# Local attention in a two-block transformer kernel: scores of two heads alternate between the array halves, VectorE adds the mask together with the maximum, and scale vectors move into the rotary tables

## The reference

```python
h = shift_token(x)                       # half the channels come from the token before
q, k, v = split(h @ wqkv)                # 8 heads of 64
q = l2norm(q) * qs; k = l2norm(k) * ksc  # t / clip(norm(t), 1e-12)
q = q * cos * scale + rotate_half(q) * sin * scale
k = k * cos / scale + rotate_half(k) * sin / scale
# windows of 128 tokens; the keys are the window before and the window itself
sim = einsum('bhwid,bhwjd->bhwij', q * 8.0, keys)
sim = where((i < j) | (i > j + 128) | (j == -1), -max_float, sim)
o = einsum('bhwij,bhwjd->bhwid', softmax(sim), values)
x = x + o @ wo
h = layernorm(shift_token(x)) * lg + lb
a, g = split(h @ w1 + b1)
x = x + (a * gelu(g)) @ w2 + b2
```

## Time and profile before

| | us |
|---|---|
| median of 3 runs | 3386.52 (3385.89 to 3389.96) |
| the profiled execution, its own time | 3379.02 |
| its span, first to last instruction | 3377.2 |
| busy: PE / PEld | 3182.4 / 2050.2 |
| busy: DVE / ACT / POOL | 2572.0 / 2144.2 / 764.8 |
| mean granted TensorE clock | 0.973 |

### The profile page before, as it was taken

One profiled execution on the slowest core, in us unless ns is written; L12 is line 12 of the kernel. 1 busy time (PEld: TensorE's weight loads), 2 busy tenths in 40 slices (PEclk: granted clock), 3 DMA queues, 4 the chain that ended last, 5 costly groups with the idle time before them and its releaser, 6 DMA issues. The chain is left out here.

```text
span 3377.2 us, 56295 instructions
## 1 busy us (share of the span) xinstructions
PE 3182.4 (94%) x20728; PEld 2050.2 (61%) x20792; DVE 2572.0 (76%) x4114; ACT 2144.2 (63%) x4870; POOL 764.8 (23%) x954
## 2 busy tenths in 40 slices
PE   8979999999999999999859999999999999999996
PEld 5633333333333333333448888888888888888885
DVE  4578888888888888886357777777777777777774
ACT  3417777777777777777745555555555556565563
POOL 4500000000000000000343333333334343343341
PEclk9959999999999999999979999999999999999998
DMA  3322222222222222222400000000000000000001
GB/s 116 129 50 39 39 38 38 38 38 38 38 38 38 34 36 32 33 38 29 144 32 1 1 0 0 0 0 0 0 1 34 1 0 0 0 0 0 0 1 68
DMA packets 47027, 97.95 MB, mean 29 GB/s; under 512 B 17184, under 2 KB 29472, under 8 KB 40480
## 3 DMA queue, kind: packets, MB, share of 16 engines
q1 hardware_dynamic: 42400, 95.48, 15.1%
q10 hardware_dynamic: 4544, 1.38, 0.2%
HBM read 71.13 MB, written 25.69 MB: 29 GB/s over the span
## 5 line engine op out<-in xcount | busy, mean ns | idle before, releaser
L653 DVE TENSOR_REDUCE mx<-aux 128x1 f32<-128x1024 f32 x1024 | 1203.6, 1219 | 169.0 <-PE aux L528 168.8
L623 ACT ACTIVATE probs<-scores 128x512 f32<-128x512 f32 x2048 | 1062.9, 604 | 312.1 <-PE scores L552 308.9
L528 PE MATMUL aux<-k_stack,q_stack 48*128 48x512 f32 x2048 | 815.1, 476 | 31.6 <-DMA k_stack<-qk_dram 18.2
L552 PE MATMUL scores<-q_stack,k_stack 50*128 50x512 f32 x2048 | 756.4, 450 | 50.7 <-ACT probs L623 24.6
L552 PEld LDWEIGHTS scores<-q_stack,k_stack 50*128 50x128 f32 x2048 | 342.7, 186 | 602.6 <-ACT probs L623 549.6
L563 PE MATMUL pv<-probs,v_ones 128*32 128x512 f32 x4096 | 551.3, 610 | 1.4 <-ACT probs L623 0.7
L528 PEld LDWEIGHTS aux<-k_stack,q_stack 48*128 48x128 f32 x2048 | 345.3, 191 | 132.9 <-DVE mx L653 68.6
L1186 PE MATMUL bank<-QO,w_sb 128*128 128x128 f32 x2816 | 333.5, 278 | 0.9 <-ACT QO L1267 0.9
L1186 PEld LDWEIGHTS bank<-QO,w_sb 128*128 128x128 f32 x2816 | 321.3, 193 | 12.1 <-issue 10.3
L494 POOL CAST m_parts<-head_max 128x16 fp32r<-128x16 f32 x32 | 6.3, 196 | 1370.8 <-DVE head_max L658 1370.8
L1199 PE MATMUL bank<-kT,wqkv_sb 64*128 64x128 f32 x1984 | 288.6, 285 | 9.5 <-issue 0.4
(11 more groups left out here) (172 smaller groups left out, 4667.7 us busy)
## 6 DMA issues: line engine op xcount, KB each, us to landing
q_stack<-qk_dram SPq DMA_DIRECT2D x192, 128.0 KB, 5.0
k_stack<-qk_dram SPq DMA_DIRECT2D x192, 128.0 KB, 6.9
qk_dram<-qkT_hi SPq DMA_DIRECT2D x32, 256.0 KB, 3.1
qk_dram<-qkT_lo SPq DMA_DIRECT2D x32, 256.0 KB, 3.6
out<-x_sb SPq DMA_DIRECT2D x9, 384.0 KB, 4.1
wqkv_sb<-in_wqkv SPq DMA_DIRECT2D x2, 1536.0 KB, 7.4
w_sb<-in_w SPq DMA_DIRECT2D x2, 1408.0 KB, 11.3
x_sb<-in_x SPq DMA_DIRECT2D x1, 2048.0 KB, 18.8
```

The source lines that it names most:

```text
L528: last = nc.tensor.matmul(aux[:, ring["unit"], block_of_keys % 2], q_stack[rows, r % BODY, tile * P:(tile + 1) * P], k_stack[rows, r % BOD ...
L552: nc.tensor.matmul(scores[:, item % BANKS1], k_stack[0:SCORE_ROWS, r % BODY, s * P:(s + 1) * P], q_stack[0:SCORE_ROWS, r % BODY, j * 512:( ...
L623: nc.scalar.activation(probs[:, item % PROBS], scores[:, item % BANKS1], ACT.Exp, scale=float(D1) ** -0.5).then_inc(probs_ready, 1)
L653: nc.vector.reduce_max(mx[:, slot, tile, half:half + 1], aux[:, unit].rearrange("p a k -> p (a k)"), AX.X).then_inc(max_taken, 1)
```

## The change

- **Scores.** The mask matmul goes. A matmul has one head against 256 keys at once, if there are two blocks. Banks are filled in pairs: a head in rows 0 to 63 into one bank, then a head in rows 64 to 127 into the other, and again. `PAIRS` is ordered for it, and kT and v keep the keys of a sequence so that both blocks are one access.
- **Mask and maximum.** For each head DVE computes (score + mask) times the inverse norm of q into `probs`, with the running minimum as second output (`tensor_tensor_reduce`). q's scale is -8 instead of 8, so the minimum is the negated maximum. ACT takes the exponential from SBUF, with scale -1.
- **Rotary.** POOL builds cosine and sine tables that hold the scale vectors, once for each pair of tiles (a position serves both sequences). DVE multiplies q and k from PSUM with the cosine table, so the separate cosine product goes. ACT copies q and k to SBUF before it squares them, and POOL's sine products wait for that copy and no longer for the norms. Only k is multiplied with its inverse norm. Before the combining adds DVE has an explicit drain.

```diff
@@ mask_and_shift
+    for keys in (slice(0, P), slice(2 * P, 3 * P)):
+        nc.gpsimd.affine_select(out=mask_sb[:, keys], in_=mask_sb[:, keys], compare_op=ALU.is_ge, fill=NO_KEY,
+                                base=0, pattern=[[1, P]], channel_multiplier=-1)
...
-NO_KEY = -1e30
-PAIRS = ((0, 2), (4, 6), (1, 3), (5, 7))
+NO_KEY, NO_SCORE = 1e30, 3e38
+PAIRS = ((0, 2), (1, 3), (4, 6), (5, 7))
@@ gpsimd
+            def rotary_tables(place, layer, position):
+
+                by_half = lambda a: a.rearrange("p a (s d) -> p a s d", s=2)
+                for table, source, scales, made in ((cos_table, cos_sb, qks_sb, cos_table_made), (sin_table, sin_sb, qks_swapped, sin_table_made)):
+                    nc.gpsimd.tensor_tensor(out=by_half(table[:, place]), in0=source[:, position].unsqueeze(2).to_broadcast([P, 2, 2, D2 // 2]),
+                                            in1=by_half(scales[:, layer]), op=ALU.mult).then_inc(made, 1)
...
-                    w.upto(norm2_made, t + 3)
+                    if st.tile_of_pair(2) == 0:
+                        w.upto(sin_table_made, st.pair(2) + 1)
+                    w.upto(qk_copied, 2 * (t + 3))
...
-                                                in1=sin_sb[:, st.position(2)].unsqueeze(2).to_broadcast([P, 2, H2, D2 // 2]),
+                                                in1=sin_table[:, st.table(2), :, lo:lo + D2 // 2].unsqueeze(2).to_broadcast([P, 2, H2, D2 // 2]),
                                                 op=ALU.mult).then_inc(sin_rnorm_made, 1)
+                    w.upto(norm2_made, t + 3)
...
+                if st.exists(3) and st.tile_of_pair(3) == 0:
+                    rotary_tables(st.table(3), st.layer(3), st.position(3))
@@ tensor
-                    for j in range(4):
-                        out = begin(f"S{j}", t + 1)
-                        nc.tensor.matmul(out[:], identb[:], mask_sb[:].rearrange("p a k -> p (a k)"), start=True, stop=False, skip_group_check=True)
-                        for u, h in enumerate(PAIRS[j]):
-                            rows = slice(h % 2 * D2, (h % 2 + 1) * D2)
-                            for kb in range(1 if st.first(1) else 0, 2):
-                                last = nc.tensor.matmul(out[:, (2 * u + kb) * P:(2 * u + kb + 1) * P], qT[rows, h // 2, :],
-                                                        kT[rows, st.slot(1 if kb else -1), h // 2, :], start=False, stop=(u == 1 and kb == 1), skip_group_check=True)
-                        end(last, f"S{j}")
+                    blocks = st.key_blocks(1)
+                    n_keys = P * len(blocks)
+                    for both in ((0, 1), (2, 3)):
+                        outs = [begin(f"S{j}", t + 1) for j in both]
+                        for u in range(2):
+                            for j, out in zip(both, outs):
+                                h = PAIRS[j][u]
+                                rows = slice(h % 2 * D2, (h % 2 + 1) * D2)
+                                at = 2 * u * P + blocks[0] * P
+                                last = nc.tensor.matmul(out[:, at:at + n_keys].rearrange("p (b k) -> p b k", k=P), qT[rows, h // 2, :],
+                                                        kT[rows, st.slot(1) % 2, blocks[0]:blocks[-1] + 1, h // 2, :], start=True, stop=True)
+                                if u == 1:
+                                    end(last, f"S{j}")
@@ scalar
                         src = item(name, t + 2)
+                        nc.scalar.copy(qk[:, a], src[:]).then_inc(qk_copied, 1)
                         nc.scalar.activation(squares[:, a], src[:], ACT.Square).then_inc(squares_made, 1)
...
-                            last = nc.scalar.activation(probs[:, j, u, b0:], src[:, u * 2 * P + b0:(u + 1) * 2 * P], ACT.Exp,
+                            last = nc.scalar.activation(probs[:, j, u, keys], probs[:, j, u, keys], ACT.Exp, scale=-1.0,
                                                         bias=negmax[:, j, u:u + 1], accum_out=sums[:, j, u:u + 1])
@@ vector
-                        nc.vector.tensor_tensor(qk[:, a].rearrange("p (h d) -> p h d", d=D2), bank(name)[:].rearrange("p (h d) -> p h d", d=D2),
-                                                qks_sb[:, st.layer(2), a].unsqueeze(1).to_broadcast([P, H2, D2]), ALU.mult).then_inc(by_dve, 1)
+                        nc.vector.tensor_tensor(qk_cos[:, a].rearrange("p (h d) -> p h d", d=D2), bank(name)[:].rearrange("p (h d) -> p h d", d=D2),
+                                                cos_table[:, st.table(2), a].unsqueeze(1).to_broadcast([P, H2, D2]), ALU.mult).then_inc(by_dve, 1)
...
-                    w.upto(sin_rnorm_made, 3 * (t + 2) + 1)
-                    nc.vector.tensor_tensor(qk_cos[:].rearrange("p a (h d) -> p a h d", d=D2 // 2), qk[:].rearrange("p a (h d) -> p a h d", d=D2 // 2),
-                                            cos_sb[:, st.position(2)].unsqueeze(2).to_broadcast([P, 2, 2 * H2, D2 // 2]), ALU.mult).then_inc(cos_made, 1)
+                    dve.drain().then_inc(cos_made, 1)
...
+                    nc.vector.tensor_tensor(qk_rot[:, 0], qk_cos[:, 0], qk_sin[:, 0], ALU.add)
+                    nc.vector.tensor_tensor(qk_cos[:, 1], qk_cos[:, 1], qk_sin[:, 1], ALU.add).then_inc(rot_made, 1)
...
-                        nc.vector.tensor_reduce(negmax[:, j], src[:, :, P if st.first(1) else 0:], AX.X, ALU.max, negate=True).then_inc(max_made, 1)
+                            last = nc.vector.tensor_tensor_reduce(out=probs[:, j, u, at:at + n_keys], in0=src[:, 2 * u * P + at:2 * u * P + at + n_keys],
+                                                                  in1=mask_sb[:, mask_at:mask_at + n_keys], scale=rnorm[:, st.slot(1, 2), h:h + 1], scalar=NO_SCORE,
+                                                                  op0=ALU.add, op1=ALU.min, accum_out=negmax[:, j, u:u + 1])
+                        last.then_inc(max_made, 1)
...
-                        nc.vector.tensor_tensor(qk_rot[:].rearrange("p a (h d) -> p (a h) d", d=D2), qk_cos[:].rearrange("p a (h d) -> p (a h) d", d=D2),
-                                                rnorm[:].unsqueeze(2).to_broadcast([P, 2 * H2, D2]), ALU.mult).then_inc(rotary_done, 1)
+                        nc.vector.tensor_tensor(qk_rot[:, 1].rearrange("p (h d) -> p h d", d=D2), qk_cos[:, 1].rearrange("p (h d) -> p h d", d=D2),
+                                                rnorm[:, st.slot(2, 2), H2:].unsqueeze(2).to_broadcast([P, H2, D2]), ALU.mult).then_inc(rotary_done, 1)
```

More of the change, by code:

```diff
@@ L70, in slot, with current, key_blocks, tile_of_pair @@
         return (self.t + d) % n
+    def current(self, d):
+        return self.slot(d) // 2
+    def key_blocks(self, d):
+        return (self.current(d),) if self.first(d) else (0, 1)
+    def tile_of_pair(self, d):
+        return (self.t + self.skipped + d) % 2
+    def table(self, d):
+        return (self.t + self.skipped + d) // 2 % 2
+    def pair(self, d):
+        return (self.t + d) // 2
 class Waiter:
@@ L1024, in feed_forward_phase @@
         squares_made, norm2_made, sin_rnorm_made = sem("squares_made"), sem("norm2_made"), sem("sin_rnorm_made")
+        qk_copied, scales_made, cos_table_made, sin_table_made = (sem(n) for n in ("qk3_copied", "scales_made", "cos_table_made", "sin_table_made"))
         cos_made, rot_made = sem("cos3_made"), sem("rot3_made")
@@ L1046, in _ @@
             w.on(norm2_made, 1), w.on(hmv_made, 1)
-            w.on(norm2_floor, 1), w.on(var_made, 1)
+            w.on(norm2_floor, 1), w.on(var_made, 1), w.on(qk_copied, 2)
+            w.on(sin_table_made, 1, lambda step: step.exists(2) and step.tile_of_pair(2) == 0)
             w.on(fmv_made, 1, last_layer(-2)), w.on(fvar_made, 1, last_layer(-2))
@@ L1138, in _ @@
                         for u in range(2):
-                            for kb in range(1 if st.first(0) else 0, 2):
+                            for kb in st.key_blocks(0):
                                 last = nc.tensor.transpose(out[:, (2 * u + kb) * P:(2 * u + kb + 1) * P], probs[:, j, u, kb * P:(kb + 1) * P], ident[:])
@@ L1169, in _ @@
                     out = begin("oT", t)
+                    blocks = st.key_blocks(0)
                     for c in range(4):
-                        for kb in range(1 if st.first(0) else 0, 2):
+                        for kb in blocks:
                             for half in range(2):
@@ L1174, in _ @@
                                 last = nc.tensor.matmul(out[half * D2:(half + 1) * D2, c * P:(c + 1) * P],
-                                                        v_sb[:, st.slot(0 if kb else -2), (2 * c + half) * D2:(2 * c + half + 1) * D2], PT[:, j, u, kb],
-                                                        start=(kb == 0 or st.first(0)), stop=(kb == 1), tile_position=(0, half * D2))
+                                                        v_sb[:, st.slot(0) % 2 + 2 * kb, (2 * c + half) * D2:(2 * c + half + 1) * D2], PT[:, j, u, kb],
```

(9 more changed lines are left out.)

51 lines of the change are left out of this document (29 added, 22 removed).

## The result

| | before | after |
|---|---|---|
| median, us | 3386.81 (3385.89 to 3389.96, 4 runs) | 3256.26 (3249.47 to 3260.75, 4 runs) |
| ratio to before, 95% interval | | 0.9611 (0.9592 to 0.963) |
| span of the profiled execution | 3377.2 | 3247.7 |
| one tile on TensorE in the first layer | 25.03 | 23.04 to 23.06 |

The kernel became 130.6 us faster; 185 were forecast. The gain arose in the forecast place, the score stage. Three tenths of it did not arrive, because of a wait that the forecast did not have.

What follows compares the result with a forecast made beforehand. TensorE, 99.4% busy in the second block's layers, was taken as the bound. 60 tiles x (3.44 - 0.12) = 199, plus 3 for first tiles, less 17 for loop turns: 185 saved, 3386.5 to 3201 us; range 3170 to 3270.

Steps and rivals of the forecast that it cites:

- TensorE bounds the layers: Second block's layers: TensorE busy 99.4%, so every microsecond leaving its queue is gained until another engine becomes late.
- Why the stage is short: Score stage on TensorE: 16 records with array halves overlapping, 5.64 us down to 2.2, saving 3.44 a tile.
- The reading of L1174: Existing f32 products alternating between array halves of columns: 32 records in 1.90 us, 0.059 each, taken as sign of overlap.
- no overlap: Rival for the score stage: halves run one after the other, 4.1 us, saving 1.54 a tile; 3292; chance 0.08.
- The fused pairs: DVE's eight mask-and-maximum instruction pairs per tile: 0.45 us each, between bounds of 0.41 and 0.54.
- full durations: Rival: each instruction of a DVE pair holds it for its whole duration, 0.58 us; stall 1.16; 3263; chance 0.10.
- half rate: Rival: the fused DVE instruction runs slower, 0.70 us a pair; stall 2.12 us; 3322; chance 0.09.
- DVE as the bound outright: Rival: DVE pairs cost over 0.83 us, using up the gain; at 1.0 us 3468; slower has chance 0.04.
- The stall: TensorE's q matmul waits for DVE's xT_lo, done at 10.29 us against 10.17 wanted: 0.12 us a tile.
- The turns: At 12 loop turns DVE stands 1.31 us before xT_lo; 1.39 us exposed each, 17 us given back.
- Other edits at nothing: Cosine product, halved k product, drain, ACT copies and POOL products: no gain or loss; up to 1 us a tile if uncovered.
- The fill: Pipeline start: a little shorter by the rotary chain; with the drain of the pipeline, longer by DVE's chain, set at nothing.

Runs made afterwards that it cites:

- e4: The changed kernel plus two reductions of 128x1024 with unused output on DVE, where the cosine product was; 3252.9 us, ratio 0.9624.
- e1: The changed kernel with DVE's last sum (F's) moved up to just behind the residual sum Y; 3186.2 us, ratio 0.9404.
- e2: The changed kernel with score products of one bank after the other instead of banks in pairs; 3248.5 us, ratio 0.9604.
- e3: The changed kernel with score products of one bank after the other and F's sum moved up behind Y's; 3183.7 us, ratio 0.9408.
- e11: The changed kernel with F's sum moved up, score products in pieces of 128 keys and one bank after the other; 3223.8 us, ratio 0.9524.

## Why the prediction was right or wrong

- **TensorE bounds the layers, and what leaves its queue is gained: right.** The stage and its entry saved 3.59 us a tile; 3.44 were forecast.
- **Why the stage is short: right.** 2.2 us were forecast from overlap of the halves, 1.93 were measured. The sign that the forecast named, records of the two halves at the same start, is there: 0.007 us apart in the kernel after. The reading of L1174 was right too; its records start in pairs, 0.109 us from pair to pair. The forecast was 0.3 too long because it took 0.24 for a record in place of 0.216 and gave the first one no partner. The rival "no overlap", 3292, is out. But the forecast's sign for it, a period above 23 us without the wait at xT_lo, did come (23.05), for another reason: the wait at the shift.
- **The fused pairs: right, a little cheaper than the low bound.** 0.405 us a pair; 0.45 was taken from 0.41 to 0.54. The low bound was the row of the same width plus that of a 128x1 instruction. The rule of the Trainium skill ("VectorE: DVE Perf Modes", "The DRAIN you can't avoid"), read as the prediction reads it, disagrees with this trace as well: an instruction of 0.47 us is followed after 0.40. The same section adds that a next operation that is not held starts earlier; the trace agrees with that. The rivals of full durations and half rate are out, and DVE as the bound outright with them: e4. That the measured 3256 lies near the price of full durations, 3263, is chance.
- **The stall: this is the step that failed.** The forecast asked only when DVE is done with xT_lo, and found it 0.12 us late. It did not walk the banks: what else does TensorE wait for between the scores and the q product? The shift wants bank 3, which F's sum frees, 2.1 us of TensorE earlier than xT_lo is wanted. Put into the forecast's own sum, DVE would be done with F's sum at 1.53 + 8 x 0.45 + 0.61 + 3.54 + 0.42 = 9.7 us after the score start, and TensorE would arrive at 2.2 + 4.71 (output projection and second feed-forward product) + 1.15 = 8.1: a stall of 1.6, seen before any run. With the measured pair and stage it is 9.3 against 7.8, 1.5. It measured 1.37 and about 0.25 for the restart, 1.62 in place of 0.12: 90 us in 60 tiles.
- **The turns: mechanism there, not exposed.** 17 us were charged; in the kernel after they cost nothing, because the shift's wait gives DVE the time. In e1 TensorE waits 0.9 us at each.
- **Other edits at nothing: right.** Cosine product, copies on ACT, tables on POOL: e4 and the absence of other waits.
- **The fill: at nothing, measured 6 us gained.**

In sum the forecast's 185 is 60 x 3.32 - 17 + 3; what came is 60 x 1.97 + 9, with 3 to 4 us outside the layers and in the scatter of the medians. The stage and the pairs gave a little more than forecast and the turns cost nothing; the one missing wait outweighs all of that. That the time still fell into the forecast's range owes something to luck: the range was made wide for other reasons.

## What to carry to other kernels

When a stage on the bounding engine gets shorter, list every wait of that engine between there and the next fixed point, also those for a free bank, and set each against the release in the other engine's queue; the nearest reserve decides, not the one that has looked tight. A release that stands last in a queue for no reason is worth moving up before anything is made faster. Where two edits aim at the same cost, try each alone: here either kept the halves busy together. And before a run is read as a test of overlap, look at the starts of the records: an edit of the order may leave the overlap in place, as in e2 and e3.

## What the runs showed of the hardware

- Two f32 products on different halves of the array rows run at once: their records start 0.007 us apart, and the next two 0.216 us later (256 columns). Alone in its half a record takes as long as one on all rows, 0.112 us for 128 columns. The Trainium skill ("TensorE: Matmul & The Clock Gate", "🎯 Why this matters for your kernels") says that a matmul on few rows takes the same time as a full one and gains only by running beside another; the trace agrees on both counts, here for f32.
- The partner need not be the next record. With four records of one half in a row (e3) the other half's first one starts 0.013 us after the first; with eight in a row (e11) it starts 0.55 us after it, beside the fifth. Why the partner waits so long there is open. With a product on all rows between them, the mask before bank 6 in the kernel before, nothing overlaps.
- Going into and out of the 64-row form costs about 0.1 us each: in the kernel after 0.31 us from the first pair to the second and from the last to the output projection, where 0.216 lie between the others.
- The fused DVE instruction (add, scale, running minimum, 256 columns) starts every 0.345 us with a constant scale and every 0.403 with a scale read from SBUF.
